# Fused cross-attention block on one core: PSUM banks of the first attention split four and two, and one more step of lag behind the exponentials

## What is computed

```python
q = _qdq(x) @ _qdq(wq).T + bq
kv = cond @ wkv.T + bkv
k, v = jnp.split(kv, 2, axis=-1)
...
scale = 1.0 / np.sqrt(Dh)
attn = jax.nn.softmax(jnp.einsum('bnhd,bmhd->bhnm', q, k) * scale, axis=-1)
o = jnp.einsum('bhnm,bmhd->bnhd', attn, v).reshape(B, N, C)
```

## Time and profile before

| what | before |
|---|---|
| median of three runs | 3102.93 us |
| profiled execution | 3099.14 us |
| its span | 3097.4 us |
| first attention: first scores to last sum of parts | 155.74 to 507.57 us |
| busy in 300 to 350 us | TensorE 47.14, VectorE 48.95, ScalarE 46.59, POOL 6.65 us |
| scores, product on TensorE (two groups, with either stack) | 494 and 484 ns, 128 times each |
| maximum, VectorE | 681 ns, 256 times |
| exponential, ScalarE | 720 ns, 256 times |
| granted TensorE clock over the span | 0.978 |

### The profile page before, as it was taken

The page is one execution under the profiler, slowest core; times in us unless marked ns, Lnnn a source line. Parts: engine busy times, 40 slices in busy tenths (PEclk is TensorE's granted clock), DMA queues, the critical chain, the costliest instruction groups (busy, mean ns, idle before and its releaser), DMA issues. The chain is left out here.

```text
span 3097.4 us, 56330 instructions
## 1 busy us (share of the span) xinstructions
PE 2912.3 (94%) x15383; PEld 2374.2 (77%) x15414; DVE 2318.9 (75%) x4671; ACT 2079.2 (67%) x4266; POOL 1410.8 (46%) x1793
## 2 busy tenths in 40 slices
PE   7889997897999999899999899999999999899988
PEld 5677775776888877678888688888888888688855
DVE  6689998765777568767776299999999999734387
ACT  4489996413666556566666588888888888633366
POOL 4323002321000084367687377777777777442132
PEclk9999998998999999999999999999999999999999
DMA  6997763227888596545456532332322322195510
GB/s 217 290 222 181 166 168 95 65 89 248 267 281 266 166 296 207 153 132 170 142 171 188 160 99 72 100 96 76 100 87 85 99 81 92 40 321 184 180 40 35
DMA packets 402271, 474.31 MB, mean 153 GB/s; under 512 B 52212, under 2 KB 267156, under 8 KB 402100
## 3 DMA queue, kind: packets, MB, share of 16 engines
q1 hardware_dynamic: 389140, 419.72, 44.8%
q0 software_dynamic: 12960, 52.61, 5.0%
HBM read 304.30 MB, written 167.92 MB: 152 GB/s over the span
## 5 line engine op out<-in xcount | busy, mean ns | idle before, releaser
L2873 POOL TENSOR_SCALAR h_probs<-h_exp,h_rowsum_inv 128x512 f32<-128x512 f32 x512 | 355.6, 695 | 275.8 <-PE h_pT L2721 259.9
L2801 DVE TENSOR_REDUCE h_neg_max<-h_scores 128x1 f32<-128x512 f32 x512 | 349.5, 683 | 141.0 <-PE h_scores L2713 140.8
L2763 ACT ACTIVATE h_exp<-h_scores,h_neg_max 128x512 f32<-128x512 f32 x512 | 355.3, 694 | 108.7 <-DVE h_neg_max L2801 100.2
L2814 DVE TENSOR_TENSOR h_probsT_lo<-h_pT,h_probsT_hi 128x512 fp32r<-128x512 f32 x512 | 348.6, 681 | 0.0
L2721 PEld LDWEIGHTS h_pT<-ident,h_probs 128*128 128x128 f32 x2048 | 253.6, 140 | 70.6 <-POOL h_probs L2873 1.8
L2721 PE MATMUL h_pT<-ident,h_probs 128*128 128x128 f32 x2048 | 306.7, 272 | 0.9 <-POOL h_probs L2873 0.8
L2772 ACT CAST h_probsT_hi<-h_pT 128x512 fp32r<-128x512 f32 x512 | 300.6, 587 | 0.9 <-PE h_pT L2721 0.9
L2995 PE MATMUL k_acc<-k_w_hi,k_cat 128*128 128x512 f32 x512 | 201.5, 394 | 12.8 <-POOL k_w_lo L3114 10.6
L2736 PE MATMUL h_pO<-h_probsT_hi,n_lo 128*128 128x512 f32 x512 | 203.3, 397 | 0.0
L2996 PE MATMUL k_acc<-k_w_lo,k_cat 128*128 128x512 f32 x512 | 200.7, 392 | 0.0
L930 ACT ACTIVATE b_probs<-b_scores,b_neg_max 128x512 f32<-128x512 f32 x256 | 184.2, 720 | 5.8 <-DVE b_neg_max L957 5.8
(11 more groups left out here) (475 smaller groups left out, 9015.1 us busy)
## 6 DMA issues: line engine op xcount, KB each, us to landing
e_w_raw<-in_w SPq DMA_DIRECT2D x24, 1792.0 KB, 8.1
lnT<-g_out SPq DMA_DIRECT2D x160, 256.0 KB, 2.3
n_raw<-lnT SPq DMA_DIRECT2D x64, 512.0 KB, 5.1
e_w_raw<-in_w SPq DMA_DIRECT2D x24, 896.0 KB, 10.1
n_raw<-lnT SPq DMA_DIRECT2D x64, 256.0 KB, 5.2
n_raw<-v SPq DMA_DIRECT2D x64, 256.0 KB, 5.5
cat<-h_cat SPq DMA_DIRECT2D x128, 128.0 KB, 1.8
k_cat<-cat SPq DMA_DIRECT2D x128, 128.0 KB, 4.8
```

What stands on the lines that cost most here:

```text
L2763: nc.scalar.activation(Pr[:, r % 4], pS[r % 2][:], ACT.Exp, bias=nmax[:, r % 4:r % 4 + 1], accum_out=rsum[:, r % 4:r % 4 + 1]).then_inc(ex ...
L2801: v.tensor_reduce(nmax[:, r % 4:r % 4 + 1], pS[r % 2][:], axis=AX, op=ALU.max, negate=True).then_inc(nmax_done.sem, 1)
L2814: v.tensor_tensor(PTl[:, br * HPG + h, :, bass.ts(q, P)], pT[r % 4][:], PTh[:, br * HPG + h, :, bass.ts(q, P)], ALU.subtract).then_inc(lo_ ...
L2873: nc.gpsimd.tensor_scalar(Pn[:, r % 4], Pr[:, r % 4], rinv[:, r % 4:r % 4 + 1], 1.0, ALU.mult, ALU.mult).then_inc(norm_done.sem, 1)
```

## The change

SB becomes 4 and TB becomes 2, so PSUM is still full with eight banks. In the lists of all three engines every function except `scores`, `maxima` and `exps` gets one more step of lag. Nothing else is touched.

```diff
-    SB, TB = 3, 3
+    SB, TB = 4, 2
...
-            pipeline(pe, N, 2 * UN, [(transposes, 3), (scores, 0), (values, 9), (o_transposes, 10)])
+            pipeline(pe, N, 2 * UN, [(transposes, 4), (scores, 0), (values, 10), (o_transposes, 11)])
...
-            pipeline(act, N, 2 * UN, [(high, 3), (exps, 1), (o_copy, 9)])
+            pipeline(act, N, 2 * UN, [(high, 4), (exps, 1), (o_copy, 10)])
...
-            pipeline(dve, N, 2 * UN, [(low, 4), (maxima, 0), (sum_parts, 10)])
+            pipeline(dve, N, 2 * UN, [(low, 5), (maxima, 0), (sum_parts, 11)])
```

## The result

The changed kernel took 3122.03 us in the median of four runs (3118.78 to 3124.17), the kernel before 3100.26 us on the same chip; the ratio is 1.0066, with a 95% interval of 1.0054 to 1.0079, so some 20 us slower (0.0066 x 3100). Forecast were 15.6 us more, 3116 us. The profiled execution took 3118.78 us.

What follows compares the result with a forecast made beforehand. VectorE was taken as the bound, losing almost only its wait for the transposed output. 14.4 us for 29 pairs plus 1.2 of filling made 15.6 us more; on the 3100.7 us mean that gave 3116 us, range 3109 to 3130.

Steps and rivals of the forecast that it cites:

- The bound and the mechanism: First attention: VectorE sets the pace; two banks make TensorE wait each step for the low part of VectorE's step just before.
- the signs: Transposes wait for low parts in nearly every step, sums start 11.0 to 11.3 us apart, ScalarE's wait for transposes grows.
- The term of 14.4 us: First to thirtieth sum of the first attention: 323.0 us after the change against 308.59 before, 14.4 us more.
- This sum waited for nothing: The sum of parts at 288.93, 10.42 us after the one before, was taken as free of any wait.
- the floor of 41.68 us per turn: VectorE's own work in a loop turn of four pairs, 4 x 10.42 us, against 42.50 us in the profile.
- Filling, 1.2 us: Between first scores and first sum, the extra lag costs one more step, 1.2 us, once.
- Draining, nothing: Behind the thirtieth sum at 490.92 nothing is added, with 0.6 us either way for one low part.
- All distances stay: Extra lag: low part, high part, copy, product and sum move together by one step; only distances to scores, maxima, exponentials grow.
- Four banks for scores, nothing: Scores may start earlier, but VectorE doesn't wait for scores in the steady part, so worth nothing by itself.
- ScalarE did not become the bound: Rival: wake-ups lengthen ScalarE's step from 1.15 to 1.25 us, 13 us on top, 3129 us; chance 0.05.
- The clock in the steady part: Rival: TensorE's clock falls in a tenth of the steps, 21 us on top, 3137 us; chance 0.03.
- The faster case: Rival: the new wait costs nothing and the turn's waits go, if low part to transposes is 0.20; 3096 to 3099, chance 0.08.

Runs made afterwards that it cites:

- banks_only: The kernel before with only the banks split anew, four for scores and two for transposed probabilities, at the old lags; ratio 1.0042 to the kernel before.
- wait_only: The kernel before, banks three and three, with only the transposes' wait made to ask for the low part of two items before; ratio 1.0044 to the kernel before.
- both_first: The changed kernel with the output's copy ahead of the exponential and the output's transposes ahead of the next pair's product; ratio 0.9989 to the kernel before.
- old_lag_both: banks_only with the output's transposes ahead of the product and the copy ahead of the exponential; 3093.64 us, ratio 0.9966 to the kernel before.
- lag_only: The changed kernel with banks put back to three and three, so only the extra step of lag remains; ratio 1.0023 to the kernel before.
- before_out_first: The kernel before with the output's transposes ahead of the next pair's product on TensorE; ratio 0.9985 to the kernel before.

## Why the prediction was right, point by point

**The bound and the mechanism** held. VectorE sets the pace, its wait for the output's transposes is what the change moves, and the two banks for transposed probabilities are why (banks_only, wait_only). The sums start 11.07 to 11.25 us apart, the transposes wait in nearly every step, and ScalarE's waits for them rise from 24.6 to 37.5 us (150 to 530 us), as the signs asked. Link by link: low part to transposes 0.83 (0.83 carried over from the turn), 0.66, 0.48, 0.68 (0.67), and from the copy to the product 0.83 or 0.84 where it is a group's first and 0.63 or 0.64 otherwise. The term of 14.4 us for the 29 pairs between the first and the thirtieth sum measured 15.0 (507.21 - 183.61 = 323.60, against 308.59).

**One link was sized by kind of pair where it shouldn't have been.** I had 0.90 for the product at a turn and 0.83 for that of the other group. The rows after show 11.24 us ahead of every second sum and 11.07 ahead of the others, so no difference between the two groups; over a turn the errors cancel to 0.07 us.

**"This sum waited for nothing"** was wrong, and with it the floor of 41.68 us per turn and the statement that at most 0.82 us a turn can be won. The floor is 41.1 to 41.2 (both_first, old_lag_both), the kernel before waited for 0.13 us even in its "free" pairs, and 1.3 us a turn were to be won. It didn't move the forecast, since the sum was made by when the chain ends, from the rows' start times. The 9.2 us in 16 waits "over the stage" were those up to 505 us; with the last sum they are 12.7 in 17.

**Filling, 1.2 us**, was mis-sized: the first sum is at 28.96 us after the first scores (26.59 before), 2.4 us later. The 1.20 of a step was taken from the steady part. But this step is run behind the wait for the second stacks, at half clock in this kernel as in the one before, and takes 1.9 us; the other 0.5 is that the stacks were there that much later. **Draining, nothing**: 523.17 - 507.21 = 15.96, as before (506.88 - 490.92). So 15.0 + 2.4 = 17.4 us in the stage, where 15.6 were forecast.

**"All distances stay"** for the lag was true of the distances and wrong as a costing: where three banks don't divide the turn, the lag moves the pair's last step into the wait of the turn (lag_only, 3.4 us in the steady turns and 6.3 in the stage). In the change this can't be seen, as four and two divide 32. **"Four banks for scores, nothing"** held (wait_only against banks_only: turns of 44.6 and 44.7 us).

**The rest of the difference**, 3 us, lies behind the stage and is not accounted for; that the stages behind shift as they are is therefore not shown by this pair of profiles.

**The rivals.** ScalarE did not become the bound, its idle time grew. The clock in the steady part stayed at 1.00, with a late weight load in nearly every step; so the rule of the Trainium skill, page "TensorE: Matmul & The Clock Gate", section "A second HAM failure mode: psum-queue depth-cycling", that short idle times between groups of matmuls can make the clock swing, isn't borne out by this kernel's waits of some tenths of a microsecond. The page saw it in bf16 products, these are fp32. The faster case was rightly held unlikely, but the point at which I let it turn was not the only one: I asked how short the link from low part to transposes would have to be, and didn't ask what else on the chain could give. Two exchanges in the order take 0.6 us and more off it and lead there (both_first, 5.7 us under the kernel before), without touching that link.

## What to carry to other kernels

In this kernel a ring with a bank less cost nothing once its user's lead wasn't needed; look for the one place in the period where the lead is used up, here the pair's output, and count from the new wait along the chain to the engine that sets the pace. A wait that occurs once a turn, because a ring doesn't divide it, is a free measurement of what it would do in every step. Before a bank or a lag is changed, try the order of the few instructions on that chain: it was worth more than either here, and took no memory. And look at the clock at the start of a stage in both kernels before a difference there is put down to the change.

## What the runs showed of the hardware

An idle time of 0.00 can hide a wait. An instruction of 0.18 to 0.20 us frees VectorE after 0.11 for the next, so a sum that starts 0.24 behind it has waited, without idle time shown. Distances of starts tell it.

How late an engine starts behind what it waits for depends on more than the instruction it waits for. From the start of the output's copy to the product that waits for it, it is 0.63 us in the middle of a group, but 0.83 where the product also has the loads of V to check, and 0.82 for the output's transposes, which check for their bank too. That further checks cost the difference isn't tried by itself, and they can't be all of it: after a turn of the loop the same product took 0.90 in the kernel before and 0.83 in the changed one.

The length of a wait alone didn't tell what the clock did behind it. TensorE waited for the second stacks for 2.20 us in banks_only and 3.22 in before_out_first, and the granted clock of the next 6 us stayed at 1.00. It waited 2.22 in wait_only and 2.64 in old_lag_both, and the clock of the window 180 to 183 us, right behind, was 0.72 and 0.70. After 3.34 us in the kernel before and 4.46 in the changed one it was 0.50 up to 183 us.
